# A mixture-of-experts step on one core: the first of two transposes of `hid` moves into the middle of the next tile's first layer

## The chip, the cores and the metric

The kernel runs on one core of a Trainium2 chip. The metric is device time in microseconds (us) of one execution; lower is better. The engines of the core are TensorE (PE in the rows, its weight loads PEld), VectorE (DVE), ScalarE (ACT), GpSimd (POOL) and SyncE (SP); each works through its own instructions in order, and they wait for one another by semaphores.

## What is computed

`x` has 4096 tokens (64 x 64) of 512 numbers. A conditioning step multiplies each batch entry by a matrix chosen by its subject, and a mixture of 16 experts follows, of which each token uses 4, plus one expert that all tokens share. The result is added to the step's input:

```
w = weights[subjects]
out = jnp.einsum('bct,bcd->bdt', x, w) + bias[subjects][:, :, None]
...
y = silu(x @ g.T) * (x @ u.T) @ d.T            # one expert; widths 512 -> 256 -> 512
acc = acc + we[:, None] * y                    # we: the token's weight for it
...
return (out + shared).reshape(B, S, H)
```

## The kernel before, in words

Tokens are taken in tiles of 128. After conditioning and the logits (to about 51 us) comes the shared expert for 32 tiles, in groups of four, beside the routing (to about 188 us). Then come `NR` = 143 routed tiles: rows gathered from `h_rows` by an index list that sorts tokens by expert, one expert per tile.

A product in float32 is made of three in a format with fewer bits: high part by high weights, high by low weights, low by high weights. So the first layer of a routed tile (`gate_up`, gate and up side by side, 512 columns, four slices of the input) is 12 matmuls into `psGU`, and the second (`down`, two slices of the hidden 256) is 6 into `psY`. Both go through `split_product` (L1107 to L1114, recorded as L1112).

Between the layers, for tile t:
- ACT makes `silu(gate)` (L935) from `psGU`; DVE multiplies it by `up` and the token's weight into `hid` (`mix`, L1759). In the rows `silu` and `hid` are parts of `aT`.
- TensorE transposes the two halves of `hid` into the bank `psH`, there is only one of it (`xpose_hid`, L1095; the instructions are recorded as L983 in the helper `transposes`).
- ACT copies `psH` to `hidT_hi` (L832, `copy_hidT`), DVE subtracts that from `psH` into `hidT_lo` (L1750, `split_hid`). Only then is `psH` free: this raises `hidT_ready`.

The order on TensorE is written by hand in `step` (L1215): first layer of tile t, the two transposes of tile t-1, second layer of tile t-2. The transposes wait for `hid_ready` (mix of t-1) and for `hidT_ready` (split of t-2, which has freed `psH`). DVE's order in a step is mix of t, split of `hid` of t-1, split of the input of t+2 (L1678), turn of the input of t+3 (L1744), and, in tiles where the next expert's weights are due, one or more pieces of the weights' low parts (`next_weights`, L1772, after ACT has made the high parts, L907). ACT: silu of t, copy of `psH`, copy of the input (L756), copy of `psY` (L841), pieces. `run_tiles` runs 14 routed tiles of TensorE ahead of a loop of 16 tiles a turn and one behind it. In the first routed tile the last second layers of the shared expert stand where the transposes would; the last tile has an order of its own.

Of the kernel before, what the change touches and what calls it, by code (L numbers as in the profile page):

```python
# [14 lines left out]
P = 128  # L15
# [7 lines left out]
HK, IK = H // P, I // P  # L23
UP = HK * 2 * I
# [115 lines left out]
def build(nc, x, x_pairs, itok, fside, cond_w, gate_w, expert_bias, ffn_w, out):  # L140
# [4 lines left out]
    with ExitStack() as ctx:  # L145
        def sb(name, shape, dt=F32):
            return ctx.enter_context(nc.sbuf_tensor(name, shape, dt))

        def ps(name):
            return ctx.enter_context(nc.psum_tensor(name, [P, 512], F32))  # L150

        def sem(name):
            return ctx.enter_context(nc.semaphore(name))

        ident = sb("ident", [P, P])
# [42 lines left out]
        xT_hi, xT_lo = xT_pair[:, 0:2, :], xT_pair[:, 2:4, :]  # L199
        silu, hid = aT[:, :, 0:I], aT[:, :, I:2 * I]  # L200
        hidT_hi = sb("hidT_hi", [P, 2, I], F32R)
        hidT_lo = sb("hidT_lo", [P, 2, I], F32R)
# [115 lines left out]
        psGU = [ps(f"psGU{i}") for i in range(2)]  # L318
        psY = [ps(f"psY{i}") for i in range(2)]
        psH = ps("psH")  # L320
# [61 lines left out]
        gu_done = sem("gu_done")  # L382
        silu_ready = sem("silu_ready")
        hid_ready = sem("hid_ready")
        hid_xposed = sem("hid_xposed")
        hidT_ready = sem("hidT_ready")
        down_done = sem("down_done")
# [578 lines left out]
        def _(pe):  # L966
# [14 lines left out]
            def transposes(dst, src, parts):  # L981
                for k in range(parts):
                    mm = pe.transpose(dst[:, k * P:(k + 1) * P], src[:, k * P:(k + 1) * P], ident[:])  # L983
                return mm
# [107 lines left out]
                pe.matmul(psT[1][:, NRP:2 * NRP - 1], limits[:], running[:], start=True, stop=True  # L1092
                          ).then_inc(limits_spread, 1)

            def xpose_hid(t, n):  # L1095
                pe.wait_ge(hid_ready, t.done(1))
                if n is None or n >= 1:
                    pe.wait_ge(hidT_ready, t.done())
                transposes(psH, hid[:, t.slot % 2, :], IK).then_inc(hid_xposed, 1)

            def weights(t, n):

                word = pe.value_load(pe_word[0:1, bass.ds(t.done(-NT), 1)])
                at = pe.snap((word >> 6).with_bounds(min_val=0, max_val=SPLITS - 1) * (2 * EW))
                return lambda col: split_w[:, bass.ds(at + col, H)], word & 63

            def split_product(dst, high, low, slot, parts, w, col):  # L1107

                for k in range(parts):
                    c = slice(k * P, (k + 1) * P)  # L1110
                    for a, at in ((high, 0), (high, EW), (low, 0)):
                        mm = pe.matmul(dst, a[:, slot, c], w(at + col + k * H), start=(k == 0 and a is high and at == 0),  # L1112
                                       stop=(k == parts - 1 and a is low))
                return mm  # L1114

            def gate_up(t, n, w, needed):
                if needed is not None:
                    pe.wait_ge(low_done, needed)
                pe.wait_ge(xT_ready, t.done(1))
                if n == NT:  # L1120
                    pe.wait_ge(silu_ready, NT)
                else:
                    pe.wait_ge(hid_ready, t.done(-1))
                split_product(psGU[t.slot % 2][:], xT_hi, xT_lo, t.slot % 2, HK, w, 0).then_inc(gu_done, 1)

            def down(t, n, w):
                pe.wait_ge(hidT_ready, t.done(1))
                if n is None or n >= 2:
                    pe.wait_ge(y_ready, t.done(-1))
                split_product(psY[t.slot % 2][:], hidT_hi, hidT_lo, t.slot % 2, IK, w, UP).then_inc(down_done, 1)  # L1130

            def fill_slots(g):

# [24 lines left out]
            def shared_down(g, j):  # L1158

                n = GROUP * g + j  # L1160
                if j == 0:
                    pe.wait_ge(hidT_ready, GROUP * (g + 1))
                if n >= 2:
                    pe.wait_ge(y_ready, n - 1)
                token = slice(j * P, (j + 1) * P)
                for c in range(IK):
                    low = shared_hid_low(g, c)
                    for a, at in ((shared_hid_high(g, c), 0), (shared_hid_high(g, c), EW), (low, 0)):
                        w = at + UP + c * H
                        mm = pe.matmul(psY[n % 2][:], a[:, token], split_w[:, w:w + H], start=(c == 0 and a is not low and at == 0),  # L1170
                                       stop=(c == IK - 1 and a is low))
                mm.then_inc(down_done, 1)
# [41 lines left out]
            kept = []  # L1214

            def step(t, n, j):
                if j == 0:
                    kept.clear()
                at, needed = weights(t, n)
                kept.append(at)  # L1220
                if n == LAST:
                    down(t + -2, n - 2, weights(t + -2, n - 2)[0])
                    xpose_hid(t + -1, n - 1)
                    gate_up(t, n, kept[-1], needed)
                    return
                gate_up(t, n, kept[-1], needed)
                if n == NT:
                    for k in range(GROUP):
                        shared_down(NT // GROUP - 1, k)
                else:  # L1230
                    xpose_hid(t + -1, None if n is None else n - 1)
                if n is None or n >= NT + 2:
                    down(t + -2, None if n is None else n - 2,
                         kept[-3] if j >= 2 else weights(t + -2, None if n is None else n - 2)[0])

            def xpose_last_hid():

# [5 lines left out]
            def last_downs(w, last_w):  # L1243
# [19 lines left out]
                mm.then_inc(down_done, 1)  # L1263

            run_tiles(pe, *PE_FFN, step)
            last_downs(weights(tile_at(LAST - 1), LAST - 1)[0], kept[-1])

# [679 lines left out]
```

## Time and profile before

| | us |
|---|---|
| median of 3 runs | 825.34 (824.69 to 826.1) |
| the profiled execution, its own time | 825.98 |
| its span in the profile | 824.2 |
| TensorE busy | 811.2 (98%) |
| VectorE, ScalarE, GpSimd busy | 484.9, 388.9, 433.2 |

The profile is one execution. The busy time of an engine is the union of its instructions; on TensorE they overlap, so what one costs is read from the distance of two starts and not from its duration. Granted clock is 0.997 of full speed on the mean. Rows of a timeline give the start in us, the time from the first start to the last end of the instructions that are merged in it, the engine, the line, and the count.

### The profile page before, as it was taken

The numbers are of one execution on the slowest core, as the hardware profiler recorded it, in microseconds if no ns is written. First come the engines' busy times: TensorE is split into PE (matmuls) and PEld (weight loads), VectorE is DVE, ScalarE is ACT, GpSimd is POOL, SyncE is SP. The second block draws the span as 40 slices with busy tenths as digits, with TensorE's granted clock in tenths as the row PEclk, the third lists the DMA queues.
The fourth block names the chain that finished last, engine by engine and source line by source line (L and its number), as shares of the span: only waits on it lengthen the run. The fifth ranks groups of instructions, "written<-read, shape, count | busy, mean of one in ns | idle before, by whom it ended". The sixth has DMA issues, their size and how long they took to land.

```text
span 824.2 us, 19365 instructions
## 1 busy us (share of the span) xinstructions
PE 811.2 (98%) x4133; PEld 650.2 (79%) x4134; DVE 484.9 (59%) x1017; ACT 388.9 (47%) x782; POOL 433.2 (53%) x399
## 2 busy tenths in 40 slices
PE   9999999999999999999999999999999999999996
PEld 5568778888887888888888888888888878888884
DVE  5788899627444446644457446647567456464541
ACT  4864334435344345534455445546455455354432
POOL 5503111635566556566565666555654664765533
PEclk9999999999999999999999999999999999999998
DMA  8985967999999899899998999998998999999955
GB/s 291 392 332 172 252 141 217 250 218 268 229 255 236 166 198 179 202 284 234 185 192 193 281 225 189 210 286 173 244 262 183 273 237 217 235 196 174 191 70 73
DMA packets 145305, 181.52 MB, mean 220 GB/s; under 512 B 30570, under 2 KB 103922, under 8 KB 142834
## 3 DMA queue, kind: packets, MB, share of 16 engines
q0 software_dynamic: 37776, 89.08, 52.5%
q1 hardware_dynamic: 106528, 80.45, 37.6%
q10 hardware_dynamic: 834, 10.49, 3.6%
q14 instruction: 150, 1.23, 0.5%
q8 instruction: 17, 0.28, 0.1%
HBM read 82.52 MB, written 67.17 MB: 182 GB/s over the span
## 4 chain that ended last, share of the span: by engine, by line
PE 94%; DVE 2%; DMA 1%; issue 1%; ACT 0%; POOLq 0%; POOL 0%; DVEq 0%; ACTq 0%; SPq 0%
PE psGU L1112 47%; PE psY L1112 24%; PE psY L1170 5%; PE psH L983 4%; PE psGU L1153 3%; PE psGU L1154 3%; PE psGU L1155 3%; PE psT L983 1%; DMA x_ring<-x_pairs 1%; PE psY L1032 1%; PE psGU L1032 1%; PE psH L1009 1%; PE psM L1140 1%; PE psM L969 0%; DVE top L1605 0%
## 5 line engine op out<-in xcount | busy, mean ns | idle before, releaser
L1112 PE MATMUL psGU<-split_w,xT_pair 128*128 x1716 | 414.6, 390 | 0.2 <-issue 0.2
L1112 PEld LDWEIGHTS psGU<-split_w,xT_pair 128*128 128x128 f32 x1716 | 321.9, 188 | 69.5 <-issue 0.7
L695 POOL DMA_INDIRECT out<-y_ring,idx_all x143 | 226.8, 1586 | 206.1 <-SPq L584 186.8
L1759 DVE SCALAR_TENSOR_TENSOR aT<-aT,w_ring,psGU 128x256 f32<-128x256 f32 x143 | 68.6, 479 | 237.0 <-ACT aT L935 144.6
L690 POOL DMA_INDIRECT tok_ring<-h_rows,idx_all x143 | 151.3, 1058 | 70.3 <-issue 42.3
L1112 PE MATMUL psY<-split_w,hidT_hi 128*128 x564 | 187.6, 413 | 0.4 <-issue 0.4
L935 ACT ACTIVATE aT<-psGU 128x256 f32<-128x256 f32 x143 | 55.0, 385 | 253.1 <-PE psGU L1112 188.7
L841 ACT ACTIVATE y_ring<-psY 128x512 f32<-128x512 f32 x173 | 103.6, 599 | 99.2 <-PE psY L1112 45.0
L1112 PE MATMUL psY<-split_w,hidT_lo 128*128 x282 | 111.2, 394 | 0.0
L1112 PEld LDWEIGHTS psY<-split_w,hidT_hi 128*128 128x128 f32 x564 | 95.4, 189 | 13.6 <-issue 0.8
L1744 DVE STREAM_TRANSPOSE psT<-x_ring 128x512 f32<-128x512 f32 x143 | 102.4, 716 | 3.6 <-DMA w_ring<-tok_ring 3.6
L1678 DVE TENSOR_TENSOR xT_pair<-psT,xT_pair 128x512 fp32r<-128x512 f32 x143 | 97.3, 680 | 4.3 <-ACT xT_pair L756 2.3
L756 ACT ACTIVATE xT_pair<-psT 128x512 fp32r<-128x512 f32 x143 | 86.5, 605 | 2.9 <-issue 2.4
L703 POOL DMA_DIRECT2D out<-y_ring x32 | 29.6, 1141 | 92.5 <-ACT y_ring L841 90.7
L1772 DVE TENSOR_TENSOR split_w<-raw_w,split_w x42 | 51.5, 1226 | 31.8 <-ACT split_w L907 23.9
L1112 PEld LDWEIGHTS psY<-split_w,hidT_lo 128*128 128x128 f32 x282 | 52.9, 188 | 12.1
L1750 DVE TENSOR_TENSOR hidT_lo<-psH,hidT_hi 128x256 fp32r<-128x256 f32 x142 | 59.2, 417 | 3.0 <-ACT hidT_hi L832 3.0
L983 PEld LDWEIGHTS psH<-ident,aT 128*128 128x128 f32 x284 | 39.5, 140 | 20.1 <-issue 1.9
L983 PE MATMUL psH<-ident,aT 128*128 128x128 f32 x284 | 54.2, 272 | 1.1 <-issue 1.1
L832 ACT ACTIVATE hidT_hi<-psH 128x256 fp32r<-128x256 f32 x142 | 53.9, 380 | 2.2 <-PE psH L983 2.1
L907 ACT ACTIVATE split_w<-raw_w x42 | 44.6, 1062 | 7.1 <-issue 2.4
L1154 PE MATMUL psGU<-split_w 128*128 128x512 f32 x96 | 37.4, 390 | 0.0
(268 smaller groups left out, 652.3 us busy)
## 6 DMA issues: line engine op xcount, KB each, us to landing
x_ring<-tok_ring SPq DMA_DIRECT2D x284, 128.0 KB
raw_w<-ffn_w SPq DMA_DIRECT2D x17, 1536.0 KB, 9.8
out<-y_ring POOLq DMA_DIRECT2D x32, 256.0 KB
x_ring<-x_pairs SPq DMA_DIRECT2D x12, 512.0 KB, 8.4
h_rows<-tok_ring SPq DMA_DIRECT2D x16, 256.0 KB, 9.7
h_rows<-y_ring SPq DMA_DIRECT2D x16, 256.0 KB, 10.4
tok_ring<-h_rows,idx_all POOLq DMA_INDIRECT x143
out<-y_ring,idx_all POOLq DMA_INDIRECT x143
```

The lines of the kernel that those rows point to most:

```text
L690: pool.indirect_dma_start(tok_ring[:, r % RING, :], None, h_rows[:, :], bass.IndirectOffsetOnAxis(idx_all[:, r:r + 1], 0)).then_inc(gather ...
L695: pool.indirect_dma_start(out[:, :], bass.IndirectOffsetOnAxis(idx_all[:, r:r + 1], 0), y_ring[:, r % YRING, :], None, compute_op=ALU.add) ...
L756: act.activation(xT_hi[:, t.slot % 2, :], psT[t.slot % 2][:], ACT.Copy).then_inc(xhi_ready, 1)
L841: act.activation(y_ring[:, s, :], psY[t.slot % 2][:], ACT.Copy).then_inc(y_ready, 1)
L935: act.activation(silu[:, t.slot % 2, :], psGU[t.slot % 2][:, 0:I], ACT.Silu).then_inc(silu_ready, 1)
L983: mm = pe.transpose(dst[:, k * P:(k + 1) * P], src[:, k * P:(k + 1) * P], ident[:])
L1112: mm = pe.matmul(dst, a[:, slot, c], w(at + col + k * H), start=(k == 0 and a is high and at == 0), stop=(k == parts - 1 and a is low))
L1154: pe.matmul(as_low, split_w[:, w:w + P], low, start=False, stop=False)
L1678: v.tensor_tensor(xT_lo[:, t.slot % 2, :], psT[t.slot % 2][:], xT_hi[:, t.slot % 2, :].bitcast(F32), ALU.subtract).then_inc(xT_ready, 1)
L1744: v.transpose(psT[t.slot % 2][:].rearrange("p (k b j) -> p k j b", k=HK, j=QUADS), x_duo[:, t.slot // DUO_TILES, :, t.slot % DUO_TILES, :] ...
L1750: v.tensor_tensor(hidT_lo[:, t.slot % 2, :], psH[:, 0:I], hidT_hi[:, t.slot % 2, :].bitcast(F32), ALU.subtract).then_inc(hidT_ready, 1)
L1759: v.scalar_tensor_tensor(out=hid[:, half, :], in0=gate, scalar=w_ring[:, w_slot, bass.ds(expert, 1)], in1=up, op0=ALU.mult, op1=ALU.mult). ...
```

## The change

Half of `xpose_hid`, the first transpose with its two waits, is issued within the first layer of the next tile, ahead of its third slice (after 6 of its 12 matmuls). The second transpose stays behind that layer, and alone raises `hid_xposed`. In the first routed tile and in the last one the order is as before; it changes in the 141 tiles between.

```diff
-            def xpose_hid(t, n):
+            def xpose_first(t):
                 pe.wait_ge(hid_ready, t.done(1))
-                if n is None or n >= 1:
-                    pe.wait_ge(hidT_ready, t.done())
-                transposes(psH, hid[:, t.slot % 2, :], IK).then_inc(hid_xposed, 1)
+                pe.wait_ge(hidT_ready, t.done())
+                pe.transpose(psH[:, 0:P], hid[:, t.slot % 2, 0:P], ident[:])
+
+            def xpose_second(t):
+                pe.transpose(psH[:, P:2 * P], hid[:, t.slot % 2, P:2 * P], ident[:]).then_inc(hid_xposed, 1)
+
+            def xpose_hid(t):
+                xpose_first(t)
+                xpose_second(t)
...
                 for k in range(parts):
+                    if k in between:
+                        between[k]()
...
-                gate_up(t, n, kept[-1], needed)
                 if n == NT:
+                    gate_up(t, n, kept[-1], needed, {})
                     for k in range(GROUP):
                         shared_down(NT // GROUP - 1, k)
-                else:
-                    xpose_hid(t + -1, None if n is None else n - 1)
+                    return
+                gate_up(t, n, kept[-1], needed, {2: lambda: xpose_first(t + -1)})
+                xpose_second(t + -1)
                 if n is None or n >= NT + 2:
                     down(t + -2, None if n is None else n - 2,
...
```

TensorE, third routed tile, from the first matmul of its first layer to the first of the second layer of the tile two before. Before:

```order
L1112 ISA [waits hid_ready,xT_ready,low_done]
L1112 MATMUL psGU0<-split_w,xT_pair 128x512
...
L1112 ISA
L1112 MATMUL psGU0<-split_w,xT_pair 128x512 x2
L983 MATMUL psH<-ident,aT 128x128 [waits hidT_ready,hid_ready]
L983 MATMUL psH<-ident,aT 128x128
L1112 ISA [waits y_ready,hidT_ready]
L1112 MATMUL psY0<-split_w,hidT_hi 128x512
```

The same place in the changed kernel, where the lines have moved by 8 (L1120 is L1112):

```order
L1120 MATMUL psGU0<-split_w,xT_pair 128x512 x2
L1098 MATMUL psH<-ident,aT 128x128 [waits hidT_ready,hid_ready]
L1120 ISA
L1120 MATMUL psGU0<-split_w,xT_pair 128x512
L1120 ISA
L1120 MATMUL psGU0<-split_w,xT_pair 128x512 x2
L1120 ISA
L1120 MATMUL psGU0<-split_w,xT_pair 128x512
L1120 ISA
L1120 MATMUL psGU0<-split_w,xT_pair 128x512 x2
L1101 MATMUL psH<-ident,aT 128x128
L1120 ISA [waits y_ready,hidT_ready]
```

The transpose that carries both waits now stands six matmuls earlier, with address work and matmuls of the same layer queued behind it; the other one is alone between the layers. No engine but TensorE has another order, and the number of instructions is the same.

## Rows read from the trace of the kernel before

**Rows 1.** The profile's page: engines, the chain that ended last, two groups
```profile
PE 811.2 (98%) x4133; PEld 650.2 (79%) x4134; DVE 484.9 (59%) x1017; ACT 388.9 (47%) x782; POOL 433.2 (53%) x399
...
PE 94%; DVE 2%; DMA 1%; issue 1%; ACT 0%; POOLq 0%; POOL 0%; DVEq 0%; ACTq 0%; SPq 0%
...
L1772 DVE TENSOR_TENSOR split_w<-raw_w,split_w x42 | 51.5, 1226 | 31.8 <-ACT split_w L907 23.9
...
L983 PE MATMUL psH<-ident,aT 128*128 128x128 f32 x284 | 54.2, 272 | 1.1 <-issue 1.1
```

**Rows 2.** Timeline of TensorE over one routed tile: start, us, line, tiles, count
```profile
504.89 0.38 PE L983 MATMUL psH<-ident,aT 128*128 128x128 f32 x2
505.03 0.71 PE L1112 MATMUL psY<-split_w,hidT_hi 128*128 x2
...
506.50 2.89 PE L1112 MATMUL psGU<-split_w,xT_pair 128*128 x12
509.23 0.38 PE L983 MATMUL psH<-ident,aT 128*128 128x128 f32 x2
```

**Rows 3.** Timeline: sixteen short matmuls between long ones, shared part
```profile
128.58 0.71 PE L1140 MATMUL psM<-entry,x_ring 128*128 128x72 f16 x16
129.13 0.48 PE L1153 MATMUL psGU<-xT_pair,split_w 128*128 128x512 f32 x1
129.44 0.39 PE L1154 MATMUL psGU<-split_w 128*128 128x512 f32 x1
...
130.60 0.39 PE L1153 MATMUL psGU<-xT_pair,split_w 128*128 128x512 f32 x1
...
131.28 0.39 PE L1153 MATMUL psGU<-xT_pair,split_w 128*128 128x512 f32 x1
```

**Rows 4.** Timeline: the same after three short matmuls
```profile
76.24 0.48 PE L1153 MATMUL psGU<-tok_high,split_w 128*128 128x512 f32 x1
...
77.71 0.39 PE L1153 MATMUL psGU<-tok_high,split_w 128*128 128x512 f32 x1
```

**Rows 5.** Timeline: an ordinary tile, split of `hid` and the first layer beside it
```profile
501.75 0.41 DVE L1750 TENSOR_TENSOR hidT_lo<-psH,hidT_hi 128x256 fp32r<-128x256 f32 x1
...
502.16 2.90 PE L1112 MATMUL psGU<-split_w,xT_pair 128*128 x12
```

**Rows 6.** Timeline: a tile in which DVE makes a piece of weights
```profile
504.83 1.23 DVE L1772 TENSOR_TENSOR split_w<-raw_w,split_w  x1 [1.43 <-ACT split_w L907]
...
507.04 0.42 DVE L1750 TENSOR_TENSOR hidT_lo<-psH,hidT_hi 128x256 fp32r<-128x256 f32 x1
```

**Rows 7.** Timeline: two tiles with a late split of `hid`
```profile
324.34 2.89 PE L1112 MATMUL psGU<-split_w,xT_pair 128*128 x12
...
325.38 0.42 DVE L1750 TENSOR_TENSOR hidT_lo<-psH,hidT_hi 128x256 fp32r<-128x256 f32 x1
...
760.33 2.91 PE L1112 MATMUL psGU<-split_w,xT_pair 128*128 x12
...
761.62 0.42 DVE L1750 TENSOR_TENSOR hidT_lo<-psH,hidT_hi 128x256 fp32r<-128x256 f32 x1
```

**Rows 8.** Timeline: tile 17 of the routed part (from 0), TensorE waits
```profile
262.73 2.90 PE L1112 MATMUL psGU<-split_w,xT_pair 128*128 x12
...
265.06 0.41 DVE L1750 TENSOR_TENSOR hidT_lo<-psH,hidT_hi 128x256 fp32r<-128x256 f32 x1
...
265.62 0.41 PE L983 MATMUL psH<-ident,aT 128*128 128x128 f32 x2
...
265.95 0.73 PE L1112 MATMUL psY<-split_w,hidT_hi 128*128 x2
...
267.85 0.95 PE L1112 MATMUL psGU<-split_w,xT_pair 128*128 x3 [0.24 <-issue]
```

**Rows 9.** Timeline: tile 111, DVE waits for a transfer, then TensorE for DVE
```profile
671.61 0.73 DVE L1744 STREAM_TRANSPOSE psT<-x_ring 128x512 f32<-128x512 f32 x1 [3.60 <-DMA w_ring<-tok_ring]
...
675.29 0.41 PE L983 MATMUL psH<-ident,aT 128*128 128x128 f32 x2 [1.10 <-issue]
...
676.13 0.73 PE L1112 MATMUL psY<-split_w,hidT_hi 128*128 x2 [0.43 <-issue]
...
677.61 2.68 PE L1112 MATMUL psGU<-split_w,xT_pair 128*128 x11
```

More of the change, by code:

```diff
@@ L1105, in weights, with split_product @@
                 return lambda col: split_w[:, bass.ds(at + col, H)], word & 63
-            def split_product(dst, high, low, slot, parts, w, col):
+            def split_product(dst, high, low, slot, parts, w, col, between):
                 for k in range(parts):
+                    if k in between:
+                        between[k]()
                     c = slice(k * P, (k + 1) * P)
@@ L1114, in split_product, with gate_up @@
                 return mm
-            def gate_up(t, n, w, needed):
+            def gate_up(t, n, w, needed, between):
                 if needed is not None:
@@ L1123, in gate_up, with down @@
                     pe.wait_ge(hid_ready, t.done(-1))
-                split_product(psGU[t.slot % 2][:], xT_hi, xT_lo, t.slot % 2, HK, w, 0).then_inc(gu_done, 1)
-            def down(t, n, w):
+                split_product(psGU[t.slot % 2][:], xT_hi, xT_lo, t.slot % 2, HK, w, 0, between).then_inc(gu_done, 1)
+            def down(t, n, w, between):
                 pe.wait_ge(hidT_ready, t.done(1))
@@ L1129, in down @@
                     pe.wait_ge(y_ready, t.done(-1))
-                split_product(psY[t.slot % 2][:], hidT_hi, hidT_lo, t.slot % 2, IK, w, UP).then_inc(down_done, 1)
+                split_product(psY[t.slot % 2][:], hidT_hi, hidT_lo, t.slot % 2, IK, w, UP, between).then_inc(down_done, 1)
             def fill_slots(g):
@@ L1221, in step @@
                 if n == LAST:
-                    down(t + -2, n - 2, weights(t + -2, n - 2)[0])
-                    xpose_hid(t + -1, n - 1)
-                    gate_up(t, n, kept[-1], needed)
+                    down(t + -2, n - 2, weights(t + -2, n - 2)[0], {})
+                    xpose_hid(t + -1)
+                    gate_up(t, n, kept[-1], needed, {})
                     return
-                gate_up(t, n, kept[-1], needed)
                 if n == NT:
+                    gate_up(t, n, kept[-1], needed, {})
                     for k in range(GROUP):
                         shared_down(NT // GROUP - 1, k)
-                else:
-                    xpose_hid(t + -1, None if n is None else n - 1)
+                    return
+                gate_up(t, n, kept[-1], needed, {2: lambda: xpose_first(t + -1)})
+                xpose_second(t + -1)
                 if n is None or n >= NT + 2:
                     down(t + -2, None if n is None else n - 2,
-                         kept[-3] if j >= 2 else weights(t + -2, None if n is None else n - 2)[0])
+                         kept[-3] if j >= 2 else weights(t + -2, None if n is None else n - 2)[0], {})
             def xpose_last_hid():
```

## The prediction, made before the changed kernel was run

> **What bounds the kernel now.** I read the page first. TensorE is busy for 811.2 of 824.2 us and makes 94% of the chain that ended last [rows 1], so time is what TensorE's instructions cost one after the other plus its few waits. Then the timeline of TensorE over one routed tile, because the page's durations overlap and say nothing of cost: the period from transpose to transpose is 509.23 - 504.89 = 4.34 us [rows 2], and nothing in it is idle. Then the timelines around other interruptions of the long matmuls, for what a short instruction among them costs. Last the timelines of DVE beside the first layer, for how early the moved transpose could start: it waits for DVE.
>
> **The present cost of the pair.** In an undisturbed row of long matmuls three starts take 131.28 - 130.60 = 0.68 us, 0.227 each [rows 3]. Eighteen are 4.08 us, so the two transposes cost 4.34 - 4.08 = 0.26 us a tile. Where it lies: the pair is 0.38 us from first start to last end and one lasts 0.272, so their starts are 0.11 apart [rows 1, 2]; the first `psY` matmul starts 0.14 after the first transpose, thus 0.03 after the second; and the six `psY` matmuls take 506.50 - 505.03 = 1.47 us, where six undisturbed ones take 1.36. So 0.11 + 0.03 + 0.11 = 0.25, and 0.01 of rounding and a slightly later start of the first transpose.
>
> **The change, part 1: one interruption more.** The 0.11 us behind the transposes is the key. It is no matter of transposes: after sixteen tiny matmuls of 72 columns the next six long ones also take 130.60 - 129.13 = 1.47 us, of which the first alone takes 129.44 - 129.13 = 0.31 [rows 3], and after three short ones it is 77.71 - 76.24 = 1.47 again [rows 4]. Two, three or sixteen short instructions, the return to long matmuls costs 0.11. Weight loads (PEld 650 us) run beside matmuls [rows 1]; my reading is that a short matmul does not cover the load of the one behind it, and that the next few starts are still a little late. The change removes the 0.11 between the two transposes (the second one's load is now covered by the twelfth matmul), and adds a second return. A lone transpose then costs 0.03 + 0.11 = 0.14, by the other way 0.26 - 0.11 = 0.15. Two are 0.28 to 0.30, where the pair costs 0.26 (0.25 by its parts). I take 0.30 - 0.26 = +0.04 us a tile. No row shows one single short step inside a routed layer: the lower bound is 0.28 - 0.26 = +0.02, the upper 0.30 - 0.25 = +0.05; further below lies only the rival without a second return. In 141 tiles: +5.6 us (2.8 to 7.1).
>
> The Trainium skill (TensorE: Matmul & The Clock Gate, Part 2, Step-by-step) says that the next tile's weights load while this tile's matmul runs. Read plainly, it speaks for the change: each lone transpose has a long matmul ahead of it. The rows agree for the load ahead of a transpose, but the matmul behind it starts late by 0.31 - 0.23 [rows 3], so by the trace the rule hides nothing for the instruction after a short one. By the rule alone the gain would be that of the first rival.
>
> **Part 2: the waits come 1.5 us earlier.** The transpose of tile t-1 waits for mix of t-1 and, later on DVE, for the split of `hid` of t-2, which frees the one bank. Before, it is due after 12 matmuls of the first layer, now after 6, which is 6 x 0.227 = 1.36 us after the layer's start. Behind it in TensorE's queue stand the other six matmuls and all that follows. Ordinary tile: the split ends at 501.75 + 0.41 = 502.16, the new place is 502.16 + 1.36 = 503.52 [rows 5], 1.36 us to spare. Tile with a piece of weights on DVE (42 pieces, [rows 1]): the piece ends at 506.06, the split at 507.46, the new place is 506.50 + 1.36 = 507.86, 0.40 to spare [rows 2, 6]. In some of these tiles, and in a few others, it is later: 325.80 for a place at 325.70, and 762.04 for a place at 761.69 [rows 7]. Going through all tiles in this way, the split ends within 0.32 us of the new place or behind it in 14 tiles; the last by rank that count have 0.28 to spare, and two are the tiles 17 and 111.
>
> How long TensorE then takes is bounded by tile 17, where it does wait: the split ends at 265.47, the transpose starts at 265.62, 0.15 later, and the next long matmul at 265.95, 0.48 later instead of 0.15 + 0.14 [rows 8]. I take 3.2, nearer to the upper end, since the matmul behind the moved transpose has its address work behind the wait. What follows in such a tile, the address work and word load of the next one, has about 3 us until it is used and stays covered.
>
> Tiles 17 and 111 wait already, so only part is new. In 17 the transpose starts at 265.62 as before, then come six matmuls (1.47 with the return), the second transpose and `psY` (0.03 + 1.47), so the next first layer starts near 268.7 where it now starts at 267.85 [rows 8]: +0.9. In 111 the same from 675.29, with the 0.84 us until `psY` (0.70 over the usual 0.14) now covered by the six matmuls: near 678.4 for 677.61 [rows 9]: +0.8. Together +1.7.
>
> Later steps: `gu_done` of a tile comes 0.14 us later against the second layer, so silu and mix do too, out of 1.36 us to spare. The second transpose, which lets ACT copy `psH`, is no later against `psY`. No DMA, no other queue moves. One pair stays together in the last tile.
>
> **Sum.** 5.6 + 3.2 + 1.7 = +10.5 us. Against the profiled execution: 825.98 + 10.5 = 836.5. It lies 0.64 above the median of the runs shown, so the median expected is 825.34 + 10.5 = 835.8 us.
>
> **Rivals.**
> - *The transpose hides in the layer (faster).* If the load behind a single transpose is covered after all, the first one costs its own short step of 0.03 and no return, and the 0.11 between the pair goes: 0.03 - 0.11 = -0.08 a tile, -11.3 us; with waits as above (+4.9) 819, without 814. It decides where `psGU` matmul 7 starts 0.23 after matmul 6 plus 0.03. For it: the pair's 0.11 is real, and no row shows a lone transpose between two long matmuls. Against: the same return of 0.11 after two, three and sixteen short ones [rows 2, 3, 4].
> - *Only the return, no waits.* DVE's late tiles differ from execution to execution, or TensorE gets by with 0.15 and fewer of them: 825.34 + 5.6 = 831, with 1 or 2 us of waits 832.
> - *No difference.* The load behind each transpose costs the same 0.11 in both orders (the pair exposes the second transpose's and `psY`'s, the split order `psGU`'s and `psY`'s), with no longer tail, and waits only in tiles 17 and 111, which come from a late transfer and may not recur: +0 to +2, 826.
> - *Waits that grow.* If a late start in one tile makes the next late as well, since the sequencer must do the six matmuls' address work and the word load after the wait, part of the 42 piece tiles wait 0.2 us more: +6 on the forecast, 842. For it: after the wait in 17 even the next layer started late [rows 8]. Against: that one had no six matmuls to run in between.
>
> **Chances.** Forecast 0.52, return without waits 0.17, waits that grow 0.10, no difference 0.10, hides 0.11. A measurement of this kernel can tell 0.2%, 1.7 us, from no change. Faster by more: 0.11. Within: the no-difference case less its upper edge, 0.08. Slower: 0.81. The forecast's own range is 831.5 to 840; the whole range, 826.5 to 841.5, leaves out the hiding case, part of the no-difference case and the far end of growing waits.
>
> **What would show it.** In the changed profile a row of one transpose between two rows of six `psGU` matmuls, the seventh starting 0.03 after the transpose and the six then taking 1.47 and not 1.36 us; the period of an ordinary tile at 4.38 (4.36 to 4.39) and not 4.34. Waits of TensorE at the moved transpose in some ten tiles, all following a late split of `hid`, 3 to 5 us in total. Wrong would be: a period under 4.34 (then the first rival, and a row of long matmuls after one short step without the late start), periods right but no idle time on TensorE (the second), or waits in more than 20 tiles (the last).

## The result, and the profile after

| | before | after |
|---|---|---|
| median, us | 825.02 (4 runs, 824.07 to 826.1) | 833.52 (4 runs, 831.77 to 834.98) |
| ratio, with 95% interval | | 1.0095 [1.0061, 1.0129] |
| profiled execution, its own time | 825.98 | 834.98 |
| span | 824.2 | 833.2 |

The change makes the kernel slower by 8.5 us, 0.95%. The forecast was 835.8, range 826.5 to 841.5. The same two parts of the page as in [rows 1], after:

```profile
PE 817.7 (98%) x4133; PEld 645.7 (78%) x4134; DVE 485.2 (58%) x1017; ACT 386.2 (46%) x782; POOL 433.1 (52%) x399
...
PE 90%; DVE 3%; issue 2%; DMA 1%; ACT 1%; another core or an unknown queue 1%; DVEq 0%; ACTq 0%; POOLq 0%; POOL 0%; SPq 0%
...
L1098 PE MATMUL psH<-ident,aT 128*128 128x128 f32 x142 | 38.7, 273 | 4.5 <-DVE hidT_lo L1759 3.8
L1101 PE MATMUL psH<-ident,aT 128*128 128x128 f32 x142 | 38.6, 272 | 0.0
```

The counts are the same. TensorE is still the chain, but for 90% of it instead of 94%, and the transpose that carries the waits has 4.5 us of idle time ahead of it, where the pair had 1.1. Busy time rose too, by 6.5 us, with no instruction more: 3.7 us of it is the longer period of a tile, below, and 1.6 us a stretch at the lower clock, in the last section. VectorE's lines have moved by 9: in rows of the changed kernel mix is L1768, and L1759 is the split of `hid`.

An undisturbed routed tile of the changed kernel, as [rows 2] show it for before (start, us, line, tiles, count):

```profile
507.26 0.27 PE L1098 MATMUL psH<-ident,aT 128*128 128x128 f32 x1
507.29 1.62 PE L1120 MATMUL psGU<-split_w,xT_pair 128*128 x6
508.75 0.27 PE L1101 MATMUL psH<-ident,aT 128*128 128x128 f32 x1
508.78 0.70 PE L1120 MATMUL psY<-split_w,hidT_hi 128*128 x2
...
510.25 1.55 PE L1120 MATMUL psGU<-split_w,xT_pair 128*128 x6
511.63 0.27 PE L1098 MATMUL psH<-ident,aT 128*128 128x128 f32 x1
```

From transpose to transpose it is 511.63 - 507.26 = 4.37 us. Each lone transpose is 0.03 long from start to start, and each is followed by a slow six: 508.75 - 507.29 = 1.46 and 510.25 - 508.78 = 1.47 us, against 1.36 to 1.38 for the undisturbed six. The weight loads beside them:

```profile
507.04 0.14 PEld L1098 LDWEIGHTS psH<-ident,aT 128*128 128x128 f32 x1
507.26 1.22 PEld L1120 LDWEIGHTS psGU<-split_w,xT_pair 128*128 128x128 f32 x6
```

The transpose's own load (507.04 to 507.18) is over before the transpose starts. The load for the long matmul behind it starts with the transpose, at 507.26, and one such load takes 0.19 us (mean of 1625 loads for the first layer, 188 ns), so it ends 0.16 us after the start that is recorded for that matmul (507.29). The median distance of two starts at each place of the tile, over all tiles with undisturbed length, in thousandths of a us (G: first layer, Y: second, T: transpose), worked out from every start in the two traces:

```
before  G231 227 227 227 227 227 227 227 227 227 227 233 T109 027 Y314 231 233 235 227 231   sum 4.341
after   G235 228 232 230 227 231 T026 G314 232 231 227 227 232 T026 Y314 230 233 236 225 231   sum 4.367
```

"Tail" is used below for the starts behind such a return that are still a little over 0.227 apart. The 0.109 between the two transposes is gone, and in its place stand 0.026, a second 0.314 and more of such late starts: +0.026 us a tile, in 141 tiles +3.7 us. By place: the exchange itself is near even (314 - 227 for 109 + 27 - 26 - 26), the late starts behind the first transpose add 0.008, and 0.017 lies in the first six matmuls of the layer. Those are the end of the tail behind the second transpose, which runs through `psY` into the next layer. It does so in some tiles of the kernel before too (55 of 134, against 85 of 125 after), so the median hides a mix; by the mean of the undisturbed tiles the difference is 0.020. The rest is waits. Over 139 tiles the time over the median period is 3.3 us before and 8.6 us after: +5.3. Together 9.0, which is the difference of the two profiled executions.

Two of the ten tiles that wait, one small and the largest:

```profile
528.26 0.48 DVE L1768 SCALAR_TENSOR_TENSOR aT<-aT,w_ring,psGU 128x256 f32<-128x256 f32 x1 [0.73 <-issue]
...
528.66 0.42 DVE L1759 TENSOR_TENSOR hidT_lo<-psH,hidT_hi 128x256 fp32r<-128x256 f32 x1
...
529.22 0.30 PE L1098 MATMUL psH<-ident,aT 128*128 128x128 f32 x1
529.34 1.66 PE L1120 MATMUL psGU<-split_w,xT_pair 128*128 x6
...
684.15 0.42 DVE L1759 TENSOR_TENSOR hidT_lo<-psH,hidT_hi 128x256 fp32r<-128x256 f32 x1
...
684.71 0.30 PE L1098 MATMUL psH<-ident,aT 128*128 128x128 f32 x1 [2.14 <-DVE hidT_lo L1759]
684.83 2.07 PE L1120 MATMUL psGU<-split_w,xT_pair 128*128 x6
```

In both the split ends 0.14 to 0.15 us ahead of the transpose (528.66 + 0.42 = 529.08), so it is the split that ends the wait. The matmul behind follows after 0.12 instead of 0.03; its address work stands behind the wait in the order, which would explain it. A wait therefore costs 0.09 us more than its own length.

### The profile page after: what moved, and what is told of

It reads as the page before. It is cut to its first block, busy times and chain, and to the rows that moved or that the text cites. A ratio compares the mean times of both kernels' runs of the same rounds, so it can differ in the third digit from the quotient of the medians.

```text
span 833.2 us, 19365 instructions
## 1 busy us (share of the span) xinstructions
PE 817.7 (98%) x4133; PEld 645.7 (78%) x4134; DVE 485.2 (58%) x1017; ACT 386.2 (46%) x782; POOL 433.1 (52%) x399
## 4 chain that ended last, share of the span: by engine, by line
PE 90%; DVE 3%; issue 2%; DMA 1%; ACT 1%; another core or an unknown queue 1%; DVEq 0%; ACTq 0%; POOLq 0%; POOL 0%; SPq 0%
PE psGU L1120 45%; PE psY L1120 23%; PE psY L1178 5%; PE psGU L1161 3%; PE psGU L1163 3%; PE psGU L1162 3%; PE psH L1098 2%; PE psH L1101 2%; PE psT L983 1%; DMA raw_w<-ffn_w 1%; PE psY L1032 1%; PE psGU L1032 1%; PE psH L1009 1%; PE psM L1148 1%
## 5 line engine op out<-in xcount | busy, mean ns | idle before, releaser
L1120 PE MATMUL psGU<-split_w,xT_pair 128*128 x1716 | 435.4, 399 | 0.0
L1120 PEld LDWEIGHTS psGU<-split_w,xT_pair 128*128 128x128 f32 x1716 | 312.0, 188 | 71.1
L1768 DVE SCALAR_TENSOR_TENSOR aT<-aT,w_ring,psGU 128x256 f32<-128x256 f32 x143 | 68.7, 481 | 245.2 <-ACT aT L935 138.8
L1120 PE MATMUL psY<-split_w,hidT_hi 128*128 x564 | 188.1, 414 | 0.0
L1120 PEld LDWEIGHTS psY<-split_w,hidT_hi 128*128 128x128 f32 x564 | 95.8, 190 | 25.4 <-issue 0.5
L1120 PE MATMUL psY<-split_w,hidT_lo 128*128 x282 | 111.4, 395 | 0.0
L1120 PEld LDWEIGHTS psY<-split_w,hidT_lo 128*128 128x128 f32 x282 | 53.2, 189 | 12.3
L1759 DVE TENSOR_TENSOR hidT_lo<-psH,hidT_hi 128x256 fp32r<-128x256 f32 x142 | 59.4, 418 | 3.9 <-ACT hidT_hi L832 3.0
L1098 PE MATMUL psH<-ident,aT 128*128 128x128 f32 x142 | 38.7, 273 | 4.5 <-DVE hidT_lo L1759 3.8
L1101 PE MATMUL psH<-ident,aT 128*128 128x128 f32 x142 | 38.6, 272 | 0.0
```

Of the source, the lines that this page charges most:

```text
L1098: pe.transpose(psH[:, 0:P], hid[:, t.slot % 2, 0:P], ident[:])
L1101: pe.transpose(psH[:, P:2 * P], hid[:, t.slot % 2, P:2 * P], ident[:]).then_inc(hid_xposed, 1)
L1759: v.tensor_tensor(hidT_lo[:, t.slot % 2, :], psH[:, 0:I], hidT_hi[:, t.slot % 2, :].bitcast(F32), ALU.subtract).then_inc(hidT_ready, 1)
L1768: v.scalar_tensor_tensor(out=hid[:, half, :], in0=gate, scalar=w_ring[:, w_slot, bass.ds(expert, 1)], in1=up, op0=ALU.mult, op1=ALU.mult). ...
```

## The experiments

Each kernel was run beside the kernel before on the same chip; the ratio is that of these runs, its interval 95%. "Period" is the median of a tile in its profiled execution, "over it" what all tiles together took above that, less what some took below it.

| kernel | median, us | ratio | period | over it, us |
|---|---|---|---|---|
| before (median on the four chips, one profile) | 824.6 to 826.4 | 1 | 4.340 | 3.3 |
| changed | 833.52 | 1.0095 [1.0061, 1.0129] | 4.366 | 8.6 |
| first transpose after 3 | 841.84 | 1.0212 [1.0195, 1.0229] | 4.367 | 14.9 |
| after 9 | 826.25 | 1.0021 [1.0007, 1.0034] | 4.347 | 2.4 |
| after 11 | 822.86 | 0.9994 [0.9977, 1.0011] | 4.333 | 1.5 |
| pair after 6 | 831.34 | 1.0077 [1.0060, 1.0094] | 4.353 | 6.9 |
| two banks | 828.34 | 1.0041 [1.0023, 1.0059] | 4.367 | 5.0 |
| short low parts | 831.27 | 1.0083 [1.0058, 1.0109] | 4.367 | 6.5 |
| short low and high parts | 833.45 | 1.0095 [1.0059, 1.0130] | 4.366 | 7.0 |
| one more, in the middle | 841.90 | 1.0229 [1.0193, 1.0265] | 4.473 | 0.1 |
| one more, behind the pair | 836.96 | 1.0161 [1.0134, 1.0188] | 4.447 | 0.1 |
| pair behind the second layer | 830.71 | 1.0042 [1.0019, 1.0064] | 4.353 | 6.4 |
| same, one matmul between | 826.60 | 1.0016 [0.9993, 1.0039] | 4.333 | 7.2 |
| three matmuls between | 827.64 | 1.0017 [0.9996, 1.0038] | 4.347 | 2.1 |

**Where the first transpose stands.** `split_product` takes the place in matmuls instead of slices:

```diff
-                    if k in between:
-                        between[k]()
...
+                    for j, (a, at) in enumerate(((high, 0), (high, EW), (low, 0))):
+                        if 3 * k + j in between:
+                            between[3 * k + j]()
...
-                gate_up(t, n, kept[-1], needed, {2: lambda: xpose_first(t + -1)})
+                gate_up(t, n, kept[-1], needed, {9: lambda: xpose_first(t + -1)})
```

After 9:

> The changed kernel with the first transpose after 9 of the 12 matmuls of the first layer in place of 6. Theory (each separate interruption costs +0.026 us a tile wherever it stands, and the place sets the waits): period of an undisturbed tile 4.366 us as in the changed kernel, so 141 x 0.026 = +3.7 over before; waits at the moved transpose go from 11 tiles (6.0 us) to the two or three that wait on a late transfer, about 2 us, of which before has 1.4 to 2: 829 to 830. Rival (all of the loss is waits): 826, since nearly none are left. Rival (all of it is the interruption): 833 as the changed kernel.

After 3:

> The changed kernel with the first transpose after 3 of the 12 matmuls. Theory: the undisturbed period stays 4.366, but the place is 0.68 us earlier than in the changed kernel; from the split's ends in the trace of before some 37 tiles would wait, 17 us in sum, beside tiles 17 and 111: +3.7 + 17 + 1 to 3 = 847 (843 to 850). Rival (the interruption alone): 833, no dependence on the place.

After 11:

> The changed kernel with the first transpose after 11 of the 12 matmuls, so that one long matmul stands between the two transposes. Theory: no wait more than before; the one matmul that follows takes the 0.31 of a return, and the return after the second transpose comes as before, but the few late starts behind the first return have no room: +0.00 to +0.02 a tile less than the 4.366, 4.35 to 4.366; total 827 to 829.5. If the cost of a lone transpose is all in its return's tail (the starts 2 to 6 behind it), the period is 4.34 and the time 825.5.

The waits depend on the place as expected, though at 3 by less: 19 tiles waited 12.8 us there (37 and 17 were expected), 10 tiles 6.0 us at 6, 2 tiles 2.0 us at 9, none at 11. The rival that the place does not matter is out: 841.8, 833.5, 826.3, 822.9. All three times lie below what was expected (843 to 850, 829 to 830, 827 to 829.5), and after 9 the time is that of the rival by which all of the loss is waits (826). One reason is that the period is not 4.366 everywhere, as the theory had it. With three long matmuls between the two transposes (after 9) it is 4.347, with one (after 11) 4.333. The medians by place, first transpose after 11:

```
G227 227 227 227 227 227 227 227 227 227 233 T032 G318 T026 Y314 233 231 227 227 227   sum 4.338
```

With one matmul between, only one tail is left, and the split costs nothing against the pair (4.338 against 4.341). So the cost of the second interruption in the changed kernel is in late starts, since 0.109 is about what 0.026 and a return of 0.087 are together. After 11 the tail behind `psY` is short as well: it ends within the second layer. Rows of that kernel, where 507.74 - 507.39 = 0.35 us hold a transpose and a long matmul:

```profile
504.89 2.66 PE L1120 MATMUL psGU<-split_w,xT_pair 128*128 x11
507.39 0.28 PE L1098 MATMUL psH<-ident,aT 128*128 128x128 f32 x1
507.43 0.48 PE L1120 MATMUL psGU<-split_w,xT_pair 128*128 x1
507.74 0.27 PE L1101 MATMUL psH<-ident,aT 128*128 128x128 f32 x1
```

**Both transposes early, as a pair.** The change is `{6: lambda: xpose_hid(t + -1)}` and no `xpose_second` behind the layer.

> Both transposes after 6 of the 12 matmuls, as a pair: one interruption as before, with the waits as early as in the changed kernel. Theory: undisturbed period 4.34 as before; waits of about 5 to 6 us over 11 tiles, of which 2 are there before: +4 to +5, 829.5 to 830.5. Rival (moving into the layer costs by itself, one interruption or two): 833.

831.34, +0.77%: most of the loss without a second interruption, and 0.8 us above what was expected. Its waits were 5.7 us in 11 tiles. This shows the waits nearly by themselves. Beside them stands the period: at 4.353 it is between the two that were named (a quarter of the tiles are at 4.340 or less), since the tail behind a pair that returns into the first layer can last nine starts. And 1.6 us of the 6.9 over it are a stretch at the lower clock, as in the last section.

**One transpose more, without a wait.** In the kernel before:

```diff
+            def spare():
+                pe.transpose(psM[:, 0:P], ident[:], ident[:])
```

issued after 6 matmuls of the first layer, or right behind the pair.

In the middle:

> The kernel before, its pair of transposes in place, with one more transpose (of the identity, into a bank that nobody reads then) after 6 of the 12 matmuls in the same 141 tiles. It waits for nothing. Theory: a lone interruption costs 0.026 to the next start, 0.314 to the one behind and a tail, 0.136 us in all (0.109 of the pair's second + the 0.026 measured for the split): 141 x 0.136 = +19, 844 (843 to 845.5), and undisturbed period 4.476. Rival (the split's cost comes from what is read or from the waits, not from the interruption): +0.055 or less a tile, under 833.

Behind the pair:

> The kernel before with the same extra transpose right behind the pair, so three in a row. Theory: a short step more within one interruption costs 0.109, period 4.449, 141 x 0.109 = +15.4, 840.5; 3.5 us less than the extra one in the middle, which is what splitting costs without any wait. Rival (no return cost for a separate interruption): the same time as in the middle.

Periods 4.473 and 4.447 (4.476 and 4.449 were expected), and next to nothing over them. 0.026 us a tile is the price of a separate interruption with no wait in it, the same number as in the changed kernel, which settles that term. The places say the same too: with the extra one in the middle the first six matmuls take 1.385, behind the pair 1.360. The two medians are further apart (841.9 and 837.0) than the periods say (3.7 us); the intervals of 0.3 to 0.4% allow that. Both are lower than expected (843 to 845.5 and 840.5), because the sums were added to a median with waits in it, and these two profiles have none: 825.98 - 3.3 + 141 x 0.133 = 841.4 and 825.98 - 3.3 + 141 x 0.107 = 837.8.

```profile
506.89 1.55 PE L1117 MATMUL psGU<-split_w,xT_pair 128*128 x6
508.28 0.27 PE L1096 MATMUL psM<-ident 128*128 128x128 f32 x1
508.30 1.62 PE L1117 MATMUL psGU<-split_w,xT_pair 128*128 x6
509.76 0.38 PE L983 MATMUL psH<-ident,aT 128*128 128x128 f32 x2
```

**Which of the two waits it is.** Banks `psH` and `psM` by turns, in the transposes, in ScalarE's copy and in the split:

```diff
-                pe.wait_ge(hidT_ready, t.done())
-                pe.transpose(psH[:, 0:P], hid[:, t.slot % 2, 0:P], ident[:])
+                pe.wait_ge(hidT_ready, t.done(-1))
+                pe.transpose((psH, psM)[t.slot % 2][:, 0:P], hid[:, t.slot % 2, 0:P], ident[:])
```

> The changed kernel with the transposes of odd and even tiles in two banks, so that the moved transpose waits for the split of t-3, long past, and for mix of t-1 alone. In every waiting tile mix ended 0.33 us before the split. Theory: each of some 11 waits gets 0.3 us shorter or goes: 2.5 to 3.3 us less than the changed kernel, 830.5 to 831. Rival (mix is what ends the wait): no change, 833.5.

828.34, lower by 0.54% than the changed kernel: 4.5 us, more than the 3.3 of the forecast. Three tiles waited in its profile (17, 113, 131, for 0.4, 0.2 and 2.6 us) where ten did, and in these three the transpose follows the end of mix by 0.06 us: it was the one bank, so the split behind mix, that ended the others' waits. The profiled execution (831.78) is the slowest of its nine. In this tile the mix ends at 526.94 and the transpose is on time at 527.21, while the split of the other bank still runs:

```profile
526.46 0.48 DVE L1768 SCALAR_TENSOR_TENSOR aT<-aT,w_ring,psGU 128x256 f32<-128x256 f32 x1 [0.80 <-issue]
...
526.86 0.42 DVE L1759 TENSOR_TENSOR hidT_lo<-psM,hidT_hi 128x256 fp32r<-128x256 f32 x1
...
527.21 0.27 PE L1098 MATMUL psH<-ident,aT 128*128 128x128 f32 x1
```

**Why mix and split are late.** Both kernels are the changed one with 8 columns of each piece of weights instead of all, first in VectorE's low parts, then in ScalarE's high parts as well:

```diff
-                    v.tensor_tensor(low, raw, high.bitcast(F32), ALU.subtract).then_inc(low_done, 1)
+                    v.tensor_tensor(low[:, 0:8], raw[:, 0:8], high[:, 0:8].bitcast(F32), ALU.subtract).then_inc(low_done, 1)
...
-                    act.activation(high, raw, ACT.Copy).then_inc(high_ready, 1)
+                    act.activation(high[:, 0:8], raw[:, 0:8], ACT.Copy).then_inc(high_ready, 1)
```

Low parts:

> The changed kernel, with the low parts of the routed experts' weights made for 8 columns only of each piece, so that VectorE's 1.23 us for a piece is near 0.1 (the rest of the low parts is left out). Theory: mix and split of hid are late in most waiting tiles because of a piece ahead of them: of 6.0 us of waits at the moved transpose those of tiles 2, 33, 77, 97, 112, 114, 120 and their like shrink, those of 15, 17, 131 (no piece) stay: 2 to 3.5 us left, time 829.5 to 831. Rival (waits come from ScalarE or late transfers): as the changed kernel, 833.5.

Both:

> The changed kernel with both parts of the routed experts' weights made for 8 columns of each piece only, on ScalarE (high) and VectorE (low); the rest is left out. The kernel that shortened VectorE's part alone kept most waits: those right behind VectorE's turn of its loop (tiles 33, 97, 113) and those in which VectorE or ScalarE stood idle with its input ready (17, 131). Theory: they stay here too, the waits of other piece tiles go (2, 55, 73, 77, 86, 120, 124): 829 to 831. Rival (ScalarE's 1.06 us a piece is what delays the rest): all but 17, 112 and 131 go, under 829.

Neither gives back what was expected: 1.0083 and 1.0095, with the changed kernel at 1.0095. (The first, 831.27, is 0.3 us above its range, and its interval holds both that range's end and no change; the second gives nothing back.) By tile the waits did move. With short low parts 33, 55, 73 and 97 still wait 0.10 to 0.12 each, and 77, 114 and 120 no more; with both short all of these are gone. The waits under 0.5 us are then in tile 2, as before, and in 99, 111 and 112, where the changed kernel has none of that size. But large ones stay or come elsewhere: 1.7 us in tile 17 and 2.5 in 131 in the first, 2.4 in 17, 1.1 in 131, and 0.9 in 113 in the second. So in these profiles the pieces make only small waits, about 1 us in all, and my theory that they make most of the loss falls, as far as one profile of each can tell. The waits in 17 and 131 follow an engine that stands still with its input ready. In the kernel before, in the step of tile 17, silu of tile 16 ends at 261.69 and mix starts at 264.66; VectorE's row says that it waited for nothing the profile shows:

```profile
261.31 0.38 ACT L935 ACTIVATE aT<-psGU 128x256 f32<-128x256 f32 x1 [2.15 <-PE psGU L1112]
...
264.66 0.48 DVE L1759 SCALAR_TENSOR_TENSOR aT<-aT,w_ring,psGU 128x256 f32<-128x256 f32 x1 [5.05 <-issue]
```

The mixes of tiles 16 and 130 are late in this way in the profiles of before, of the changed kernel and of both kernels here (2.0 to 3.9 us after silu where 0.2 is usual; 1.8 to 1.9 at 130 in the first two). At 16 it is so in the profiles of all twelve kernels that leave the first transpose ahead of the second layer or inside the first, by 2.1 to 3.7 us. They stand at fixed places of the program: 16 is the first tile of VectorE's loop, 130 the third behind it. What holds the engine there was not tried and stays open.

**The other way: later.** The pair behind the second layer; then the first transpose one matmul before its end; then the first one where the pair stood and the second after 3 matmuls of the second layer.

```diff
-                else:
-                    xpose_hid(t + -1, None if n is None else n - 1)
...
                 if n is None or n >= NT + 2:
                     down(t + -2, None if n is None else n - 2,
...
+                if n != NT:
+                    xpose_hid(t + -1, None if n is None else n - 1)
```

Pair:

> The kernel before with the pair of transposes of tile t-1 behind the second layer of t-2, 1.47 us later than before. One interruption as before. Theory: undisturbed period 4.34; the waits that before has at the pair (1.4 us and the address work behind, 2 to 3 us in tiles such as 17 and 111) shrink, since the place is 1.47 us later: 822 to 823.5 where before has 824.6. Rival: the word load and address work of the next tile, which now stand right behind the waiting pair, show in every tile that waits, or ScalarE's copy, 1.4 us later, makes others late: 825 to 828.

One between:

> As the kernel with the pair behind the second layer, but the first transpose one matmul ahead of the end of that layer, so that one long matmul stands between the two. Theory: by the kernel with the first transpose after 11 of 12 (undisturbed period 4.338 by its steps against 4.341), 0.003 to 0.007 us a tile less: 0.4 to 1 us under the one with the pair, 821.5 to 823. Rival: two separate interruptions cost 0.026 a tile wherever they stand: 3.7 more, 826.

Three between:

> The first transpose right behind the first layer, where the pair stood, the second one after 3 of the 6 matmuls of the second layer. Waits as in the kernel before (place after 12). Theory (the tail of late starts behind a return is some five matmuls long, and a second interruption within it pays only the part of the tail that is left): three matmuls between give a period between that with one between (4.338) and that with six (4.366), 4.345 to 4.36; time 825.5 to 828. Rival (the split costs only by its waits): as before, 824.6.

The pair is slower, 1.0042, as its rival had it, though above the rival's range (830.71 for 825 to 828, where before has 826.39 on this chip) and in a way I had not named. The wait moves from the transposes to the second layer, which needs the split of its own tile, now made later; in tile 131 it waited 2.64 us:

```profile
766.36 0.42 DVE L1750 TENSOR_TENSOR hidT_lo<-psH,hidT_hi 128x256 fp32r<-128x256 f32 x1
...
766.92 0.72 PE L1112 MATMUL psY<-split_w,hidT_hi 128*128 x2 [2.64 <-DVE hidT_lo L1750]
```

And its period is 4.353 where 4.34 was expected, with nine late starts behind the return into the first layer. With one matmul between the transposes it is 4.333 again, which repeats the result of "after 11" at another place. By the medians this kernel is faster by 4 us than the one with the pair; the periods give 2.8, and the intervals of the two ratios overlap. It was expected 0.4 to 1 us under the pair, at 821.5 to 823, and missed that: the second layer waits here as well, for 2.1, 1.0 and 1.6 us in tiles 17, 124 and 131. Three between gives 4.347, as after 9, within the expected range, and 1.0017, which is not told from 1. Of all kernels only the one after 11 has a median under the kernel before on its chip (822.86 against 824.57), and its ratio of 0.9994 is not told from 1 either: no version here beats the kernel before for sure.

## Why the prediction was right, step by step

- *What bounds the kernel, and the pair's present cost of 0.26 us a tile.* Right: period and places are as read, before and after.
- *One interruption more, +0.04 us a tile, +5.6 us.* The mechanism is shown (the extra transpose in the middle against the one behind the pair), the size was at its lower end: +0.026 and +3.7 us. I took the pair's whole cost less 0.11 for that of a lone one, 0.15; but part of the pair's cost is a tail of six to nine starts, and the one behind the first transpose is cut off after five matmuls by the second, at a cost of 0.008. The other way of counting, 0.14 by the return alone, gives the 0.02 that was the lower bound. That the measured term is above it was not in the reasoning: 0.017 of it is the tail behind the second transpose, which reaches into the next first layer in more tiles than before. Why it does is not known.
- *The address work behind the wait.* Bounded by 0.15 and 0.32 us after the split (the rows of tile 17 give 0.48 - 0.14 = 0.34 for the upper one); measured 0.146 to the transpose and 0.095 more behind it, so 0.24, in the middle and not near the upper end.
- *Waits of 3.2 us in 12 tiles and 1.7 us more in tiles 17 and 111.* Sum 4.9, measured 5.3, partly by luck in its shares. Seven tiles with small waits (2, 33, 77, 97, 114, 120, 131) took 2.8 us over the period. The large ones took 6.0 (tiles 15, 17, 112), where before has 3.0, so +3.0 and not +1.7. The 1.7 was also high by its own terms: a transpose, six matmuls, a transpose and `psY` are 0.03 + 1.47 + 0.03 + 1.47 = 3.0 us, so +0.8 and +0.7. Tile 17 was no worse than before (0.9 over the period in both, since VectorE's stop ahead of it was 0.9 us shorter in this execution); a wait in tile 15 was new (1.1), and the largest, now in 112, took 4.0 instead of 2.0, 1.6 of it by what the last section shows. That the late tiles are those in which VectorE makes a piece was only a small part of the truth.
- *The first rival, that the transpose hides in the layer.* Out. The matmul behind each lone transpose has 0.31 and not 0.23 us until the next start, also where nothing waits. The Trainium skill's sentence that the next tile's weights load beside this tile's matmul (TensorE: Matmul & The Clock Gate, Part 2, Step-by-step) holds here for the load ahead of the transpose (507.04 to 507.18, beside the matmul before it) and not for the one behind, which starts with the transpose and needs 0.19 us where the transpose gives it 0.03.
- *Return without waits* needs 825.0 + 3.7 = 828.7 by the measured term: that is the kernel with two banks (828.3), not the changed one. *No difference* and *waits that grow* did not come: in the changed kernel no tile waited next to one that had waited.
- *The total.* +8.5 us for +10.5, inside the forecast's own range. The shares are those of one execution, the slowest of the four (834.98 for a median of 833.52); another one has other large waits, as the profiles of the kernels above show, so that their sum came near 4.9 is in part chance.

## What to carry to other kernels

Where TensorE issues long matmuls back to back, a short instruction costs less next to another short one, or one matmul away from it, than by itself: count interruptions and their tails, not instructions. A wait that is moved ahead on the engine that bounds the kernel takes its slack from all tiles, and the price is paid by the few in which another engine is late, so read the margin tile by tile and not in the ordinary one. When one bank carries two stages, look at what frees it: a second bank gave back more than half of the loss here.

## What was not expected of the hardware

The longest wait cost more than itself. In the changed kernel TensorE waited 2.3 us at 684.7; the next four matmuls started 0.23 to 0.33 apart, and then, until 689.4, most were 0.41 to 0.43 apart instead of 0.227. The granted clock (the number ahead of the last two) is 1.00 before the transpose, and lower in the two stretches behind it, in parts of which it stood at the lower level of 1.2 GHz:

```profile
680.00:684.70 4.70, 2.57 (x12) 1.77 (x11) 2.17 (x4) 1.56 (x5) 4.00 (x3) 1.00 1.09 258
684.70:687.50 2.80, 2.79 (x10) 2.24 (x11) 2.21 (x3) 1.58 (x5) 0.00 (x0) 0.71 1.23 224
687.50:690.00 2.50, 2.50 (x9) 1.98 (x8) 1.52 (x5) 1.00 (x3) 0.00 (x0) 0.65 0.18 62
```

Over nine starts it is 1.6 us, so this tile took 4.0 us more than the median: 2.3 of waiting, 0.1 behind it, 1.6 of clock. The kernel before waited 1.25 us a tile earlier (tile 111, [rows 9]) and kept its clock. Its wait had another cause: there VectorE stood for a transfer, here silu of tile 111 started at 683.14, 3.4 us behind the last matmul of its layer, where 0.04 us is usual. The pair after 6, the two banks and the pair behind the second layer show such a stretch too, once each, behind waits of 2.4, 2.6 and 2.6 us. The length of the wait alone does not decide it. With the first transpose after 3, TensorE waited 2.7 us in tile 17 and the granted clock stayed at 1.00; with short low parts it waited 2.5 us in tile 131 and with both parts short 2.4 in tile 17, and the clock stayed at 1.00 too. The rows of the first of these, with nine matmuls at the usual pace behind the wait:

```profile
267.02 0.30 PE L1098 MATMUL psH<-ident,aT 128*128 128x128 f32 x1 [2.55 <-DVE hidT_lo L1759]
267.14 2.32 PE L1120 MATMUL psGU<-split_w,xT_pair 128*128 x9
...
260.00:268.00 8.00, 5.45 (x26) 4.22 (x25) 2.56 (x5) 1.82 (x5) 4.21 (x4) 1.00 0.96 198
268.00:272.00 4.00, 4.00 (x20) 3.24 (x19) 2.00 (x5) 1.75 (x4) 1.04 (x2) 1.00 0.79 141
```

What decides it is open.
